# First attention of a two-layer transformer kernel: head groups in pairs, eight probability buffers, two copies moved to ScalarE

## The reference, cut to what matters

```python
h = layernorm(x) * (1 + ca) + sa
x_norm = layernorm(h) * gamma + beta
q = l2_normalize(heads(x_norm @ w_q))       # 16 heads of 8
k = l2_normalize(heads(x_norm @ w_k))
v = heads(h @ w_v)
resonance = 0.5 + 0.5 * tanh((q @ k.T - 0.27) * 15.0)
gate_q = 0.25 + 0.75 * sigmoid(q @ g_q)     # gate_k alike, with k and g_k
fused = (resonance * gate_q[:, None] * gate_k[None, :]) @ v
x = x + ga * (concat(fused) @ w_o + b_o)
```

## Time and profile before

| what | us |
|---|---|
| median of three runs (1302.66 to 1304.25) | 1302.71 |
| the profiled execution | 1303.03 |
| its span, first to last instruction | 1301.1 |
| mean granted clock of TensorE | 0.972 of full |
| busy: PE / DVE / ACT / POOL | 1212.8 / 1047.7 / 929.9 / 575.0 |
| first attention, 256 ACTIVATEs of line 688, busy | 270.5 |
| second attention, 256 ACTIVATEs of line 2443, busy | 248.2 |

### The profile page before, as it was taken

One profiled execution on the slowest core, in us unless ns is written; L12 is line 12 of the kernel. 1 busy time (PEld: TensorE's weight loads), 2 busy tenths in 40 slices (PEclk: granted clock), 3 DMA queues, 4 the chain that ended last, 5 costly groups with the idle time before them and its releaser, 6 DMA issues.

```text
span 1301.1 us, 37745 instructions
## 1 busy us (share of the span) xinstructions
PE 1212.8 (93%) x13717; PEld 808.6 (62%) x13717; DVE 1047.7 (81%) x2935; ACT 929.9 (71%) x1338; POOL 575.0 (44%) x793
## 2 busy tenths in 40 slices
PE   3899999999997899996999999999789999999998
PEld 2555555555544667775555555555368787878776
DVE  5899999999967787757899999999557777777763
ACT  0699999999993565542788888888557666766765
POOL 2455555555522243323343333334146566565653
PEclk6799999999999999998999999999979999999999
DMA  4311111111002122102100000000000000000000
GB/s 142 144 34 39 38 40 36 38 37 39 26 10 58 46 57 59 44 19 78 35 14 16 17 14 16 17 15 14 8 0 10 8 16 8 16 16 8 16 8 26
DMA packets 48040, 41.68 MB, mean 32 GB/s; under 512 B 5376, under 2 KB 46688, under 8 KB 47360
## 3 DMA queue, kind: packets, MB, share of 16 engines
q1 hardware_dynamic: 47872, 39.45, 10.7%
HBM read 35.09 MB, written 4.34 MB: 30 GB/s over the span
## 4 chain that ended last, share of the span: by engine, by line
PE 48%; DVE 3%; issue 1%; ACT 0%; POOL 0%; ACTq 0%; DVEq 0%; POOLq 0%
PE psum_all L2825 25%; PE psum_all L2356 9%; PE psum_all L2342 4%; PE psum_all L2123 2%; PE psum_all L2382 1%; PE psum_all L2319 1%; PE psum_all L2328 1%; PE psum_all L2368 1%; PE psum_all L2309 1%; PE psum_all L2872 1%; PE psum_all L2374 1%; PE psum_all L2683 1%; PE psum_all L2115 0%; DVE ffn_gated L2981 0%; DVE ffn_xhat L2674 0%
## 5 line engine op out<-in xcount | busy, mean ns | idle before, releaser
L2443 ACT ACTIVATE a_probs<-psum_all 128x1024 f32<-128x1024 f32 x256 | 248.2, 1022 | 67.6 <-PE psum_all L2342 67.6
L2825 PE MATMUL psum_all<-ffn_hi,weights_r 128*128 128x512 f32 x704 | 284.8, 405 | 9.3 <-issue 4.1
L688 ACT ACTIVATE probs<-psum_all,biases 128x1024 f32<-128x1024 f32 x256 | 270.5, 1114 | 26.0 <-PE psum_all L594 26.0
L2825 PE MATMUL psum_all<-ffn_lo,weights_r 128*128 128x512 f32 x704 | 278.3, 395 | 0.0
L2785 POOL TENSOR_TENSOR ffn_lo<-ffn_full,ffn_hi 128x512 fp32r<-128x512 f32 x143 | 186.8, 1314 | 135.2 <-ACT ffn_hi L2902 98.7
L2825 PEld LDWEIGHTS psum_all<-ffn_hi,weights_r 128*128 128x128 f32 x704 | 134.3, 191 | 50.8 <-issue 9.9
L2825 PEld LDWEIGHTS psum_all<-ffn_lo,weights_r 128*128 128x128 f32 x704 | 134.5, 191 | 25.9
L607 PE MATMUL psum_all<-probs,vpad 128*32 128x257 f32 x2048 | 138.9, 389 | 0.3 <-ACT probs L688 0.3
L2356 PE MATMUL psum_all<-a_probs,vpad 128*32 128x256 f32 x2048 | 137.5, 386 | 0.6 <-DVE a_sums L2521 0.6
L2914 ACT ACTIVATE ffn_full<-psum_all,scales 128x512 f32<-128x512 f32 x128 | 88.4, 690 | 68.3 <-PE psum_all L2825 68.2
L2785 DVE TENSOR_TENSOR ffn_lo<-ffn_full,ffn_hi 128x512 fp32r<-128x512 f32 x64 | 55.1, 862 | 80.4 <-ACT ffn_hi L2917 80.4
(11 more groups left out here) (232 smaller groups left out, 2620.4 us busy)
## 6 DMA issues: line engine op xcount, KB each, us to landing
a_mod_gate<-modulation_table SPq DMA_DIRECT2D x64, 128.0 KB, 2.9
X<-in_x SPq DMA_DIRECT2D x32, 128.0 KB, 3.0
a_mod_norm<-modulation_table SPq DMA_DIRECT2D x32, 128.0 KB, 3.1
f<-in_f SPq DMA_DIRECT2D x2, 2048.0 KB, 10.2
e_mod_norm<-modulation_table SPq DMA_DIRECT2D x32, 128.0 KB, 3.1
out<-X SPq DMA_DIRECT2D x16, 256.0 KB, 2.3
e_gates<-modulation_table SPq DMA_DIRECT2D x32, 64.0 KB, 2.8
weights<-in_h SPq DMA_DIRECT2D x2, 1024.0 KB, 7.7
```

What stands on the lines that cost most here:

```text
L688: nc.scalar.activation(probs[:, c % 4, :, :, 0:T].rearrange("p r k q -> p (r k) q"), SC[c % 2].rearrange("p (a q) -> p a q", q=T), ACT.Tan ...
L2443: nc.scalar.activation(probs[:, c % 4, :, :, :].rearrange("p r k q -> p (r k q)"), SC[c % 2], ACT.Exp, scale=float(np.float32(1.0) / np.sq ...
L2825: ins = nc.tensor.matmul(dst, weights[:, w0:w0 + P], part[layer][:, k, :], start=first and i == 0, stop=last and i == len(parts) - 1)
```

## The change

- *Steps.* PE's `step` puts the score chunks and head groups in pairs: scores 0, 1; `project_qk`, `turn_keys`, `turn_queries`; scores 2, 3; head groups 2 and 3 of the batch before; scores 4, 5; logits and values, `turn_gates`, `project_out`, `turn`; scores 6, 7; head groups 0 and 1. `every` makes one step less at the end.
- *Buffers.* `probs` has eight buffers. The turned queries go through the bank of the gates (PG and PP) in place of PT.
- *ACT.* It takes over the copy of `hT` and the high part (`hT_out`, `split_high`), both behind chunk 5; `square` is behind chunk 0 and `gate` behind chunk 1. The gate's tanh of the queries is written broadcast and turned as it is; its scale and bias are applied in `gT_out`. The three biases are numbers in the instruction.
- *DVE and POOL.* The order of both is new; the first norm is done for batch b+4 in step b, and the residual for b-1.

The diff, cut to its core; `@@` names the function, indentation is cut:

```diff
-tanh_bias, gate_k_bias, gate_q_bias = (biases[:, i:i + 1] for i in range(3))
+tanh_bias, gate_k_bias, gate_q_bias = -COLLAPSE * SHARPNESS, 0.625, 0.3125
-PT16 = PT.bitcast(F16)
+PT16, PG16 = PT.bitcast(F16), psum[:, 3584:4096].bitcast(F16)
+    for b in range(-3, B + 1):
@@ turn
-    wait(pe, qT_done, n - 1)
+    wait(pe, values_done, n - 1)
+    wait(pe, logits_done, n)
@@ project_logits_v
-    pe.wait_ge(hT_done, up_to(b + 3))
+    wait(pe, kT_done, up_to(b + 2))
@@ turn_keys
-    pe.wait_ge(values_done, n + 1)
-    pe.wait_ge(logits_done, up_to(n + 2))
+    pe.wait_ge(xnT_done, up_to(n + 2))
@@ turn_queries
-    pe.wait_ge(kT_done, n + 1)
+    wait(pe, x_done, n - 2)
+    wait(pe, gT_done, n - 1)
-            last = nc.tensor.transpose(PT16[:, g * T + t * P:g * T + (t + 1) * P],
+            last = nc.tensor.transpose(PG16[:, g * T + t * P:g * T + (t + 1) * P],
@@ turn_gates
-    wait(pe, gT_done, n)
+    pe.wait_ge(qT_done, up_to(n + 2))
-        last = nc.tensor.transpose(PG[:, t * P:(t + 1) * P], gate_q[p][:, t, :], ident[:, :])
+        last = nc.tensor.transpose(PG[:, t * P:(t + 1) * P], tanh_q[p][:, t, :], ident[:, :])
@@ heads
-                                    probs[:, (2 * g + r // 2) % 4, r % 2, kb, 0:UNIT],
+                                    probs[:, 2 * g + r // 2, r % 2, kb, 0:UNIT],
@@ project_out
-    pe.wait_ge(gT_done, up_to(n + 2))
@@ PE: step
-    for pair in range(CHUNKS // 2):
-        if there(b):
-            scores(b, p, 2 * pair)
-            scores(b, p, 2 * pair + 1)
-        if pair == 0:
-            if isinstance(b, int) and b == 0:
-                turn(2)
-            if there(b - 1):
-                heads(b - 1, 1 - p, G - 1)
-            if isinstance(b, int) and b == B:
-                bound_sums(pe)
-            if there(b + 2):
-                project_qk(b + 2)
-            if there(b + 2) or there(b + 1):
-                project_logits_v(b, p)
-        elif there(b):
-            heads(b, p, pair - 1)
-        if pair == 1 and there(b + 1):
-            turn_keys(b + 1, 1 - p)
-        if pair == 2:
-            if there(b + 1):
-                turn_queries(b + 1, 1 - p)
-            if there(b):
-                turn_gates(b, p)
-        if pair == 3:
-            if there(b - 1):
-                project_out(b - 1, 1 - p)
-            if there(b + 3) and not (isinstance(b, int) and b == -1):
-                turn(b + 3)
+    if there(b):
+        scores(b, p, 0)
+        scores(b, p, 1)
+    if b == 0:
+        turn(2)
+    if there(b + 2):
+        project_qk(b + 2)
+    if there(b + 1):
+        turn_keys(b + 1, 1 - p)
+        turn_queries(b + 1, 1 - p)
+    if there(b):
+        scores(b, p, 2)
+        scores(b, p, 3)
+    if there(b - 1):
+        heads(b - 1, 1 - p, 2)
+        heads(b - 1, 1 - p, 3)
+    if b == B:
+        bound_sums(pe)
+    if there(b):
+        scores(b, p, 4)
+        scores(b, p, 5)
+    if there(b + 2) or there(b + 1):
+        project_logits_v(b, p)
+    if there(b):
+        turn_gates(b, p)
+    if there(b - 1):
+        project_out(b - 1, 1 - p)
+    if there(b + 3) and b != -1:
+        turn(b + 3)
+    if there(b):
+        scores(b, p, 6)
+        scores(b, p, 7)
+        heads(b, p, 0)
+        heads(b, p, 1)
@@ ACT: gate
+    nc.scalar.activation(tanh_k[:, :].rearrange("p (t v) -> p t v", t=TT), by_kind[:, :, 1, :],
+                         ACT.Tanh, scale=0.5 / SPLIT_SCALE).then_inc(tanh_k_done, 1)
+    nc.scalar.activation(tanh_q[p][:, :, :].rearrange("p t (v d) -> p t v d", d=HD),
+                         by_kind[:, :, 0, :].unsqueeze(3).broadcast_to([P, TT, H, HD]), ACT.Tanh, scale=0.5 / SPLIT_SCALE)
+    act.wait_ge(tanh_k_done, n + 1)
-    nc.scalar.activation(gate_k[:, :], gate_tanh[:, 1, :, :].rearrange("p t v -> p (t v)"), ACT.Identity,
-                         bias=gate_k_bias, scale=0.375)
-    nc.scalar.activation(gate_q[p][:, :, :].rearrange("p t (v d) -> p (t v) d", d=HD),
-                         gate_tanh[:, 0, :, :].rearrange("p t v -> p (t v)").unsqueeze(2).broadcast_to([P, TT * H, HD]),
-                         ACT.Identity, bias=gate_q_bias, scale=0.1875).then_inc(gates_done, 1)
+    nc.scalar.activation(gate_k[:, :], tanh_k[:, :], ACT.Identity, bias=gate_k_bias, scale=0.375).then_inc(gates_done, 1)
@@ gT_out
+    wait(act, projected, n)
-    nc.scalar.copy(gT[:, :], PG).then_inc(gT_done, 1)
+    nc.scalar.activation(gT[:, :], PG, ACT.Identity, bias=gate_q_bias, scale=0.1875).then_inc(gT_done, 1)
+def hT_out(n, p):
+    act.wait_ge(turned, n + 1)
+    wait(act, vl_psum, n)
+    nc.scalar.copy(hT[p][:, :], PT[:, 0:T]).then_inc(hT_done, 1)
+def split_high(n, p):
+    act.wait_ge(qkn_done, n + 1)
+    wait(act, kstack_psum, n - 1)
+    wait(act, qstack_psum, n - 1)
+    nc.scalar.copy(part(p, 0), normed()).then_inc(hi_done, 1)
@@ prob
-    wait(act, heads_done, b * G + (c // 2 - 1))
-    nc.scalar.activation(probs[:, c % 4, :, :, 0:T].rearrange("p r k q -> p (r k) q"),
+    wait(act, heads_done, b * G - G + (c // 2 + 1))
+    nc.scalar.activation(probs[:, c, :, :, 0:T].rearrange("p r k q -> p (r k) q"),
@@ ACT: step
-        if c == 0 and there(b + 1):
-            gate(b + 1, 1 - p)
-        if c == 1 and there(b + 2):
+        if c == 0 and there(b + 2):
-        if c == 5 and there(b):
-            gT_out(b)
+        if c == 1 and there(b + 1):
+            gate(b + 1, 1 - p)
+        if c == 5:
+            if there(b):
+                gT_out(b)
+            if there(b + 3):
+                hT_out(b + 3, 1 - p)
+            if there(b + 2):
+                split_high(b + 2, p)
@@ POOL: step
-    if fresh:
-        norm_1(pool, b + 3)
+    if there(b + 3) and b != -3:
+        norm_2(pool, b + 3)
-        norm_2(pool, b + 3)
-    if isinstance(b, int) and b in (B - 2, B - 1):
+    if there(b + 4):
+        norm_1(pool, b + 4)
+    if b in (B - 2, B - 1):
@@ DVE: xnT_out, split_high, queries_out, residual
+def xnT_out(n):
+    dve.wait_ge(hT_done, n + 1)
-    nc.vector.tensor_copy(hT[p][:, :], PT[:, 0:T]).then_inc(hT_done, 1)
-def split_high(n, p):
-    nc.vector.tensor_copy(part(p, 0), normed()).then_inc(hi_done, 1)
-    nc.vector.tensor_copy(qT[p][:, :, :].rearrange("p g k -> p (g k)"), PT16).then_inc(qT_done, 1)
+    nc.vector.tensor_copy(qT[p][:, :, :].rearrange("p g k -> p (g k)"), PG16).then_inc(qT_done, 1)
+    dve.wait_ge(gT_done, up_to(n + 2))
@@ DVE: step
-    if ahead:
-        stats_1(dve, b + 3)
-    if older:
-        residual(b - 2)
-    if ahead:
-        norm_1a(dve, b + 3)
-    if old:
-        heads_out(b - 1)
-    if isinstance(b, int) and b == B:
-        bound_reduces(dve)
-    if new:
-        values(b + 1, 1 - p)
-    if next_:
-        logits_out(b + 2)
-    if ahead:
-        norm_1b(dve, b + 3)
-    newton_of(1)
-    newton_of(2)
+        queries_out(b + 1, 1 - p)
+    newton_of(1, 2)
+    if old:
+        heads_out(b - 1)
+    if b == B:
+        bound_reduces(dve)
-    if new:
-        queries_out(b + 1, 1 - p)
-    newton_of(7, 8, 9)
+    if new:
+        values(b + 1, 1 - p)
+    if next_:
+        logits_out(b + 2)
+    newton_of(7, 8, 9)
-        gate_sums(b + 2)
+    if old:
+        residual(b - 1)
+    if fresh:
+        stats_1(dve, b + 4)
+        norm_1a(dve, b + 4)
-        turned_out(b + 3, 1 - p)
+        xnT_out(b + 3)
-        split_high(b + 2, p)
+        gate_sums(b + 2)
+    if fresh:
+        norm_1b(dve, b + 4)
+sbuf["probs"] = sb0("probs", [P, CHUNKS, 2, TT, UNIT_PAD])
```

40 lines of the change are left out of this document (14 added, 26 removed).

## The result

The changed kernel takes 1337.7 us (median of 4 runs, 1336.1 to 1341.4) against 1302.9 for the kernel before (4 runs): ratio 1.0268, 95% interval 1.0248 to 1.0287. It is slower by 34.8 us; 1333 was forecast, with a range of 1313 to 1343. The profiled execution has a span of 1335.6, 34.5 longer than before.

What follows compares the result with a forecast made beforehand. A closed loop through ACT's cast, waiting for `qkn`, was taken to bound each step of the first attention: 29 x (11.95 - 10.90) = 30.5 us, start and end 0; 1302.7 + 30 = 1333 us, range 1313 to 1343.

Steps and rivals of the forecast that it cites:

- the loop: First attention, each step: scores, QK, square, DVE's chain, cast, last two probability ACTIVATEs; 11.95 us taken against 10.90.
- first four places: Starts counted from the last probability ACTIVATE's start: next step's second scores 1.07, QK 1.39, square 2.56, DVE's reduction 3.19 us.
- DVE's part: From the start of DVE's reduction to `qkn` (scaled queries and keys) ready, including POOL's power: 7.43 us.
- The stretch of the fourth Newton step: DVE's step takes 0.57 us beside POOL's bias addition, 0.202 at its shortest; the new order saves 0.36.
- no return: POOL's stretch of DVE does not reappear at the second norm's output or Newton step 7: step 11.75 us.
- full return: POOL's whole stretch of DVE reappears on the new neighbours: step 12.1 us or a little more.
- The signs: Trace evidence expected if right: steps about 12 us, named waits on ACT and DVE, probability ACTIVATEs at 1.02.
- start and end: First and last steps of the first attention: start taken as 0 within -3 and +3 us, end within the same bound.
- The length of a step before: First attention of the kernel before: 10.90 us a step, from (387.9 - 40.8 - 9.2) / 31.
- Rival 1: Loop of PE and ACT through the transposes and hT's copy decides: 11.2 to 11.3 a step, 1313 us; chance 0.11 including between.
- Rival 2: Relieved engines decide, PE the busiest sets the step: say 10.3 us, 1290 us in all; chance 0.06.
- Rival 3: PE's idle pieces lower its clock in places, QK doubles: 1 us a step there, 1345 us or more; chance 0.03.

Runs made afterwards that it cites:

- a1: The changed kernel with the cast to the high part moved on ACT behind the step's last probability ACTIVATE: 1328.5 us, ratio 1.0221.
- c1: The changed kernel with the cast to the high part back on DVE, ahead of the low part: 1325.7 us, ratio 1.0199.
- b2: The kernel before with constant biases and both copies (hT, cast) on ACT behind the last probability ACTIVATE; single head groups, old orders: 1294.0 us, ratio 0.9937.
- a3: The changed kernel with POOL's gate product and addition to X moved behind the doubling of the queries: 1323.8 us, ratio 1.0179.
- f1: b2 with the cast alone moved on ACT ahead of the last two probability ACTIVATEs: 1406.4 us, ratio 1.0813.
- g1: f1 with the copy of hT also ahead of the last two probability ACTIVATEs, before the cast: 1433.3 us, ratio 1.1025.

## Why the prediction was right, step by step

- **The waits that decide.** S1 waits for P7 of the step before, QK behind it, the cast ahead of P6: the loop exists, and its first four places came exactly where they were put (1.07, 1.39, 2.56, 3.19). a1 and c1 open it and the step falls by 0.27 and 0.42; b2 makes the same two moves off the loop and comes out 0.6% faster than before, not 2.7% slower.
- **DVE's part** was summed to 7.43 and measured 7.29, by two errors that nearly cancel. From reduction to second aggregate 3.52 was taken and 2.98 came. The stretch of the fourth Newton step went, as foreseen (0.21 for 0.57; from its start to the aggregate 0.32 for 0.59), and from the seed to its start DVE needs 0.64 in the new order, for which 0.87 was taken. From the aggregate to `a_xn` 1.46 was taken and 1.38 came. The slot of `a_xn` was taken at 0.51 plus up to 0.5, and came at 1.01: the whole stretch returned. The 11.95 was a midpoint of "no return" and "full return"; what came was the full return, in a row that is shorter elsewhere. That the sum meets the measured 11.95 so exactly is luck.
- **The signs** were right in kind and partly too large. ACT waits 0.63 for QK ahead of the square (0.7 was said) and P takes 1.02, but the cast waits only 0.23 for `qkn`, DVE only 0.4 to 0.8 for the squares (1.6 was said) and 0.21 for POOL's power (0.6 was said).
- **The shared interface.** a3 shows the return to be POOL's doing: with the gate product and the addition elsewhere `a_xn` takes 0.60 and the step is 0.50 shorter. That agrees with the Trainium skill (GPSIMD Engine Reference, Specifications), where GpSimd shares its SBUF interfaces with VectorE and contends with some of its instructions. Which of its two cases a TENSOR_SCALAR with one tile from SBUF is, no run here tells.
- **The sum.** Steps 2 to 28 cost 29.0 more (323.2 against 294.2), with 27 steps at their full length instead of 29. The first two steps cost 1.2, P0 of the first comes 0.4 later, the last two steps 0.4, the last step from P0 to P7 1.7: 32.8. The steady steps cost less than the 30.5 that was summed; start and end, taken as 0 within 3 each, made 3.7, and 1.7 came behind the attention, which was taken as unchanged. These two are the terms that were mis-sized, and they put the time 4.7 above the forecast. The trace shows where the 1.7 arises. The last projection of the second attention comes 33.0 later than before (971.29 for 938.25), and the first matmul of the last feed-forward part 35.5 later (978.47 for 943.02): PE is idle for 5.95 ahead of it where it was 4.06, released by nothing that the profile shows. This goes with the program: 5.7 to 6.1 in the five kernels with the changed order on PE, 3.2 to 4.2 in the nine with the old one. Why is open.
- **The length of a step before** was taken as 10.90 in the belief that P7 of the last step, too, starts 9.2 behind its P0 and that all steps are alike. In the last it is 7.4, and the first step takes 14.44. The two slips cancel: steps 2 to 28 took 10.90 on average.
- **Rival 1** (loop of PE and ACT with the transposes) is not the longest but close. ACT waits 0.79 for the transposes and then 0.23 for `qkn`. By the prediction's own sign (the cast waits little, `hT` waits for PE) rival 1 would hold, but that sign doesn't tell the two apart: the transposes start 9.25 behind P7 after waiting 0.59 for DVE's copy of the logits, a wait that the prediction had left out, and the logits stand in the same row of DVE as `qkn`. In a1 this wait is on the path. What keeps c1 from the 1321 that was expected is DVE's row, with `xhat` stretched to 1.32.
- **Rival 2** was wrong for this change. b2 comes near to it: with the moved work off the loop PE is the fullest engine, at 10.54 and not 10.3, though with single groups. Two head groups in sequence take 1.88 from start to start against twice 1.01. That agrees in direction with the Trainium skill (TensorEngine Tiling, Key Properties), by which a change of tiling mode drains TensorE.
- **Rival 3** was not seen in steps 2 to 28 (granted clock 1.00 in the earlier trace rows's stretch). In the last step it was: PE is idle for 1.11 and 0.52, the pair of head groups behind that takes 3.20 in place of 1.95 at half the clock, and ACT waits 2.32 for scores at 417.68. That is the 1.7 of the last step:

```profile
414.40:417.60 3.20, 3.20 (x37) 1.13 (x29) 0.45 (x1) 0.96 (x2) 0.00 (x0) 0.50 0.00 0
```

```profile
413.90 3.20 PE L611 MATMUL psum_all<-probs,vpad 128*32 128x257 f32 x32
```

f1 and g1 show what the lower level can cost in the stage: g1's steps of 14.75 and 15.97 stand beside its one step of 13.13 at the upper level.

## What to carry to other kernels

An instruction that is moved to an idle engine takes its wait with it, and everything behind it on that engine waits too: before moving one, follow the chain from the instructions behind it back to its own input, and if it closes, sum it and compare with the step. Then try such work behind the last instruction that starts the next round. In the same kernel (b2 and g1) the two copies gave a step of 10.54 there, and one of 13.1 and more ahead of P6. A stretch by a neighbouring engine is priced by where it lands, on the path or in a wait, and not by its size alone.

## What was not expected of the hardware

- POOL's stretch of DVE moves with the order but does not go away: the TENSOR_SCALAR pair of 128x128 took 0.60, 1.09, 1.32 or 1.48 beside different work of POOL, a 128x64 step 0.18 or 0.46. In b2 both pairs took 0.60.
- The granted clock in a stage of small waits. The changed kernel has PE idle for 0.4 to 0.6 at a time in its steady steps and kept 1.00. In f1 and g1 PE sits idle 1.6 and 2.0 at a time, and the mean clock falls to 0.87 and 0.84; the matmuls at the lower level stand in the piece right behind the wait, which the loop passes.
